# Block inversions in two groups of tiles, block moves by DMA, biases folded into weights, first tile of the last part by pairs

## The reference

```python
qkv = x @ gates_w + gates_b
q, k, v = jnp.split(qkv, 3, axis=-1)
lr = x @ lr_w + lr_b
k = k / jnp.linalg.norm(k, axis=-1, keepdims=True)
K = jnp.tril(jnp.einsum('ntc,nsc->nts', k, k), k=-1)
u = jax.scipy.linalg.solve_triangular(K + jnp.eye(T), v, lower=True)
score = jnp.einsum('nsk,ntk->nst', q, k)
y = jnp.einsum('nst,ntv->nsv', score, lr * u)
x = x + (y @ out_w + out_b)
x = x + relu(layernorm(x, mn_g, mn_b) @ w1 + b1) @ w2 + b2
```

## Time and profile before

| | us |
|---|---|
| median of 3 runs | 243.82 (243.53 to 244.35) |
| the profiled execution | 244.24 |
| its span in the profile | 242.4 |
| PE busy | 192.9 (80%) |
| DVE busy | 151.5 (62%) |
| ACT busy | 120.2 (50%) |
| POOL busy | 89.6 (37%) |

### The profile page before, as it was taken

How to read it: one execution, slowest core, us unless ns; L and a number is a source line. 1 busy time by engine, 2 the same in 40 slices (tenths; PEclk the granted TensorE clock), 3 DMA queues, 4 the chain that set the end, 5 groups by cost and what they waited for, 6 DMA issues and landing times.

```text
span 242.4 us, 4068 instructions
## 1 busy us (share of the span) xinstructions
PE 192.9 (80%) x1328; PEld 138.1 (57%) x1328; DVE 151.5 (62%) x626; ACT 120.2 (50%) x316; POOL 89.6 (37%) x146
## 2 busy tenths in 40 slices
PE   0499899560028799999997647999999999999981
PEld 0287777420027799889886326666565566556530
DVE  2647642899982354455540444597977869787875
ACT  2468686859412344455445145527364555545130
POOL 2538888200058815555300752201433414021120
PEclk9999999975555599999999958999999999999997
DMA  5940000000000000000000000000101001010111
GB/s 137 292 104 0 3 3 0 3 0 1 0 0 0 3 0 3 3 0 5 1 3 0 0 3 0 0 0 0 47 0 43 18 28 45 1 43 0 46 43 43
DMA packets 12133, 5.58 MB, mean 23 GB/s; under 512 B 1736, under 2 KB 12112, under 8 KB 12112
## 3 DMA queue, kind: packets, MB, share of 16 engines
q1 hardware_dynamic: 11536, 5.25, 7.8%
q10 hardware_dynamic: 576, 0.07, 0.2%
HBM read 3.22 MB, written 2.10 MB: 22 GB/s over the span
## 4 chain that ended last, share of the span: by engine, by line
PE 63%; DVE 16%; ACT 2%; issue 1%; POOL 0%; DVEq 0%
PE ps L1031 21%; PE ps L827 7%; PE ps L822 4%; DVE xi L613 4%; DVE prod L606 4%; PE ps L943 4%; PE ps L947 3%; PE ps L1008 3%; PE ps L937 3%; PE ps L951 3%; PE ps L1023 3%; PE ps L923 2%; PE ps L931 2%; DVE v_all L756 2%; PE ps L898 2%
## 5 line engine op out<-in xcount | busy, mean ns | idle before, releaser
L1031 PE MATMUL ps<-ewC,v_all 128*128 128x512 f32 x128 | 60.3, 595 | 0.8 <-DVE v_all L756 0.7
L756 DVE COPY_PREDICATED v_all<-mask,ps 128x256 f32<-128x256 int32 x112 | 48.8, 436 | 19.0 <-ACT v_all L500 11.9
L1031 PEld LDWEIGHTS ps<-ewC,v_all 128*128 128x128 f32 x128 | 22.1, 191 | 19.2 <-issue 16.5
L314 POOL TENSOR_TENSOR x_all<-x_all,v_all 128x512 f32<-128x512 f32 x7 | 8.9, 1271 | 58.1 <-ACT v_all L506 58.1
L272 POOL COPY tt_all<-dT_all 32x128 f32<-32x128 f32 x30 | 11.8, 392 | 26.7 <-DVE dT_all L618 24.9
L898 PE MATMUL ps<-tt_all,gg_all 32*32 32x32 f32 x128 | 5.2, 205 | 17.5 <-POOL tt_all L272 17.5
L306 POOL TENSOR_TENSOR h_all<-h_all,cb 128x512 f32<-128x512 f32 x8 | 10.1, 1267 | 17.4 <-DVE cb L685 17.4
L226 POOL TENSOR_SCALAR xh<-x_all,mv,rr 128x128 f32<-128x128 f32 x16 | 12.5, 793 | 9.6 <-DVE rr L557 9.1
L479 ACT ACTIVATE k_all<-h_all,nb,rr 128x128 f32<-128x128 f32 x32 | 13.7, 483 | 2.8 <-DVE nb L710 2.8
L898 PEld LDWEIGHTS ps<-tt_all,gg_all 32*32 32x32 f32 x128 | 4.3, 117 | 18.9 <-issue 18.3
L565 DVE TENSOR_TENSOR v_all<-ps,bv 128x512 f32<-128x512 f32 x8 | 5.5, 692 | 15.1 <-PE ps L844 15.1
(11 more groups left out here) (134 smaller groups left out, 453.4 us busy)
## 6 DMA issues: line engine op xcount, KB each, us to landing
x_all<-in_L_attn_x_dram SPq DMA_DIRECT2D x8, 256.0 KB, 4.5
out_dram<-x_all SPq DMA_DIRECT2D x7, 256.0 KB, 2.3
ew<-in_L_ffn_expert_w_dram SPq DMA_DIRECT2D x1, 512.0 KB
out_dram<-x_all SPq DMA_DIRECT2D x2, 128.0 KB, 1.8
wk<-in_L_attn_gates_w_dram ACTq DMA_DIRECT2D x1, 64.0 KB, 4.0
wvl<-in_L_attn_gates_w_dram SPq DMA_DIRECT2D x1, 64.0 KB, 3.8
bv<-in_L_attn_gates_b_dram SPq DMA_DIRECT2D x1, 64.0 KB, 3.4
b2s<-in_L_attn_b_dram SPq DMA_DIRECT2D x1, 64.0 KB, 4.1
```

The source lines that it names most:

```text
L756: nc.vector.copy_predicated(sel[t % 2][:, n], mask[t % 2][:, n, E - 1 - e].unsqueeze(2).broadcast_to([P, 2, F]), ps[:, b:b + 2, (e % EH) * ...
L1031: last = nc.tensor.matmul(ps[:, 4 + 2 * half + n, :], x1T[t % 2][:, 2 * pair + n], ewC[:, EH * half:EH * half + EH, :].rearrange("p e f -> ...
```

## The change

- Front: the values leave it. ACT takes one sequence of each normalised tile, POOL one and DVE two, into `h_all` (no double buffer). dn_g is multiplied into the weights (`gall`), dn_b and the biases become two small products added to the weights (`folded`) or a bias column of the keys (`kb`); the constant 1 is added to `xnT` so that the value bias comes out of the product itself. The first tile of x comes by two transfers.
- The diagonal blocks are moved by 28 transfers of SP from `gg_all` to `gd`, of tile 3 by four copies of ACT. POOL's `blocks`, `tt_` and `da_` are gone.
- The inversion runs in two groups, tiles 0 to 3 and 4 to 7. A group has 64 blocks, and each lies on two partitions, one for the even and one for the odd columns of its inverse, so a step is on (31-j) x (j//2+1) elements. The first group starts after tile 3; DVE's list has the second group's steps interleaved with the recurrence's first tiles.
- `v_` of all tiles, the preparation of the expert weights (`prep(0)` to `prep(3)`) and the joins of tiles 0 and 1 run on PE and ACT while DVE inverts; the first tile's right sides and all of these evictions are ACT's. `prep(4)` and `prep(5)` (the two centred expert products) stand in the fold.
- h is computed during the recurrence (ACT two sequences of a tile, POOL two), no longer during the inversion.
- Last learning-rate products straight from PSUM, two by ACT and two by DVE; the fold and the first tile of the last part by pairs of sequences (LOW, HIGH); the q bias through the weights, out_b as a product of one row; `cb` and `hcb_` are gone.

```diff
--- before.py
+++ after.py
...
-    def blocks(t):
...
-        for b in range(NB):
...
-            nc.gpsimd.tensor_copy(gd_all[r, :, t * NS:t * NS + NS].rearrange("p c n -> p n c"),
-                                  gg_all[r, t, :, Q * b:Q * b + Q]).then_inc(gd_done, 1)
...
-    def hcb_(t):
-        nc.gpsimd.tensor_tensor(h_all[:, t], h_all[:, t], cb[:], ALU.add).then_inc(hcb_ready, 1)
...
+    sp.dma_start(x_all[:, 0, 0:2], x_v[:, 0, 0:2]).then_inc(x_loaded[0], 16)
...
+    for t in range(T):
+        if t == TG - 1:
+            continue
+        sp.wait_ge(g_ready, t + 1)
+        for b in range(NB):
+            r = slice(Q * b, Q * b + Q)
+            sp.dma_start(gd[t // TG][r, t % TG * NS:t % TG * NS + NS, :],
+                         gg_all[r, t, :, Q * b:Q * b + Q]).then_inc(gd_sent[t // TG], 16)
...
+    pool.wait_ge(d_done, NG)
...
+    for t in range(T):
+        for n in LOW:
+            last = nc.gpsimd.tensor_scalar(h_all[:, t, n], x_all[:, t, n], mv[:, 0, t, n, 0:1], rr[:, t, 0, n:n + 1],
+                                           ALU.subtract, ALU.mult)
+        last.then_inc(h_pool, 1)
+        pool.wait_ge(h_pool, t + 1)
+        pool.wait_ge(h_act, t + 1)
+        nc.gpsimd.tensor_tensor(x_all[:, t], x_all[:, t], b2s[:, :].unsqueeze(1).broadcast_to([P, NS, C]),
+                                ALU.add).then_inc(xb2_ready, 1)
...
+    act.dma_start(x_all[:, 0, 2:4], x_v[:, 0, 2:4]).then_inc(x_half, 16)
...
-        nc.scalar.activation(rows(xnT_all[:, t]), ps[:, 0, :], ACT.Identity, bias=dnb, scale=dng).then_inc(xnT_ready, 1)
+        nc.scalar.activation(rows(xnT_all[:, t]), ps[:, 0, :], ACT.Identity, bias=onec[:, 0:1]).then_inc(xnT_ready, 1)
...
+        if t == TG - 1:
+            for b in range(NB):
+                r = slice(Q * b, Q * b + Q)
+                last = nc.scalar.copy(gd[0][r, t * NS:t * NS + NS, :], tiles(2 + t % 2)[r, :, Q * b:Q * b + Q])
+            last.then_inc(gd_act, 1)
...
+    nc.scalar.mul(gall[:, C:2 * C], wall[:, C:2 * C], dng).then_inc(scaled_k, 1)
...
+            nc.scalar.mul(bmean[:], dnb.broadcast_to([P, P]), 1.0 / C)
+            nc.scalar.mul(gall[:, 0:C], wall[:, 0:C], dng)
+            nc.scalar.mul(gall[:, 2 * C:3 * C + 1], wall[:, 2 * C:3 * C + 1], dng).then_inc(scaled_w, 1)
...
+    def diagonals(g):
+        act.wait_ge(dT_done, g + 1)
+        for b in (0, 2):
+            r = slice(Q * b, Q * b + Q)
+            nc.scalar.copy(by_block(tt_all, g, r, b), dT_all[g][r])
+        r = slice(0, Q)
+        nc.scalar.copy(by_block(da_all, g, r, 0), plain(g)[r]).then_inc(tt_act, 1)
...
+    for n in LOW:
+        act.wait_ge(w_mm, t * NS + n + 1)
+        nc.scalar.mul(ww[t % 2][:, n, C:2 * C], ps[:, n, C:2 * C], v_all[:, t, n, C:VW]).then_inc(lrw_ready, 1)
...
-    m, w = Q - 1 - j, j + 1
+    m, w = Q - 1 - j, j // 2 + 1
...
+        nc.vector.transpose(lt[:].rearrange("p c r -> p (c r)"),
+                            gd[g][:, :, :].rearrange("p t c -> p c t").unsqueeze(2).broadcast_to([P, Q, 2, GN])
+                            ).then_inc(lt_done, 1)
...
+    def place(g):
...
+        nc.vector.transpose(d_all[g][:].rearrange("p k l -> p (k l)"),
+                            xi[g][:].rearrange("p r k -> p k r")).then_inc(d_done, 1)
+        dve.wait_ge(d_done, g + 1)
+        nc.vector.transpose(dT_all[g][:].rearrange("p t r -> p (t r)"), plain(g)).then_inc(dT_done, 1)
...
+        nc.vector.tensor_copy(by_block(da_all, g, slice(Q, 2 * Q), 1), plain(g)[Q:2 * Q])
+        for b in (1, 3):
+            r = slice(Q * b, Q * b + Q)
+            last = nc.vector.tensor_copy(by_block(tt_all, g, r, b), dT_all[g][r])
+        last.then_inc(tt_dve, 1)
...
+    prepare(0)
+    eliminate(0, 0, Q - 1)
+    place(0)
+    prepare(1)
+    eliminate(1, 0, CUTS[0])
+    for n in range(NS):
+        s_(0, n)
...
+    for n in HIGH:
+        dve.wait_ge(w_mm, t * NS + n + 1)
+        nc.vector.tensor_scalar(ww[t % 2][:, n, C:2 * C], ps[:, n, C:2 * C], v_all[:, t, n, C:VW], None,
+                                ALU.mult).then_inc(lrw_last, 1)
...
+    def folded(dst, of, ready):
+        nc.tensor.matmul(dst, cent[:], gall[:, of], start=True, stop=False)
+        nc.tensor.matmul(dst, bmean[:], wall[:, of], start=False, stop=False)
+        nc.tensor.matmul(dst, oner[:], ball[:, of], start=False, stop=True).then_inc(ready, 1)
...
-    pe.wait_ge(mT_ready, 1)
...
-    nc.tensor.matmul(ps[:, 6, :], bqB[:], rows(mw[:, :, :]), start=True, stop=True).then_inc(cb_mm, 1)
-    nc.tensor.matmul(ps[:, 7, :], wqT[:], rows(mw[:, :, :]), start=True, stop=True).then_inc(gn_mm, 1)
+    for bank, of in ((7, LOW), (3, HIGH)):
+        nc.tensor.matmul(rows(tiles(bank)[:, span(of)]), oner[:], bor[:, :].unsqueeze(1).broadcast_to([1, 2, C]),
+                         start=True, stop=False)
+    for pair, of in enumerate((LOW, HIGH)):
+        pe.wait_ge(mT_ready, pair + 1)
+        four(5 + pair, lambda n: mT[:, n], lambda n: wo[:], mw_mm, of)
+    for pair, (bank, of) in enumerate(((7, LOW), (3, HIGH))):
+        pe.wait_ge(mw_ready[pair], 1)
+        nc.tensor.matmul(rows(tiles(bank)[:, span(of)]), wqT[:], rows(mw[:, span(of)]), start=False,
+                         stop=True).then_inc(gn_mm, 1)
...
```

1082 lines of the change are left out of this document (601 added, 481 removed).

## The result

The changed kernel takes **236.35 us** (median of four executions: 236.16, 236.18, 236.52 and 242.22) against 244.08 for the kernel before. The ratio is 0.969, 95% interval 0.966 to 0.972: 3.1% faster. The forecast was 224.9, with a range of 219.4 to 232.0: the direction is right, the size is not. The profiled execution has a span of 234.4, so 10.9 us are to be found against the 223.5 of the sum.

A forecast was written before the change was run, and what follows sets the result against it. GpSimd was taken to bound the front, VectorE the inversion, TensorE the recurrence and experts, dependent steps the fold. Span 242.4 - 14.5 (to w(3)) - 4.4 (fold) = 223.5; + 1.84 - 0.42 gave 224.9 us, range 219.4 to 232.0.

The forecast's parts named there:

- w(0) starts near 62.6: First tile's w products, after the joins of tiles 0 and 1: start at 62.6, its state reaching VectorE at 65.4.
- The cover: Joins and values hidden under VectorE's inversion steps: 0.6 us of slack; as a rival, 1 to 4 us late, chance 0.08.
- The clock rival: TensorE gaps from 50 to 86 keep the clock low until tile 3: 8 us more, 233; chance 0.09.
- Its second half, low through tile 7: Half clock holding through tile 7 of the recurrence as well: 19 us more, 252; chance 0.04.
- To tile 3: From the second placing's end to w(3): 5.6 us with handovers, w(3) at 85.9 instead of 100.43.
- The lt transposes: Start of each inversion group: transpose, reciprocal, scaling and one small instruction, 3.2 us for the first group, 3.3 the second.
- The placing: VectorE's transposes and three 32x512 copies after each group's inversion steps: 4.3 us, bounds 3.4 to 6.5.
- GpSimd's hold: GpSimd normalising h beside VectorE's second placing: 0.6 us added; rival 2 to 4 us more over some 23 us, chance 0.14.
- Periods of tiles 4 to 7: Recurrence tiles 4 to 7 keep TensorE's list of products, 6.68 us each, so w(7) starts at 112.6.
- Fold and first tile: From w(7) to the second expert group: 23.9 us against 28.28 by working in pairs, 4.4 gained.
- The front: Work up to the fourth tile: loop of 3.45 us per tile, first inversion starting at 27.1.
- The line for the steps: Inversion step cost: 0.28 us plus 4.7 ns per element of width, at least 0.46; 15.7 for 31 steps.

The follow-up runs named there:

- fill_first_gap: Changed kernel plus 14 filler products of 128x128 on TensorE between the third preparation and ya(0); 233.6 to 236.0 us, ratio 0.958.
- values_ahead: Changed kernel with value tiles 4 and 5 moved ahead of ya(0), 6 and 7 one step earlier; 233.4, 233.9, 234.3 us, ratio 0.952.
- in_order: values_ahead, tile3_by_scalare, blocks_in_a_row together, value tile 5's eviction behind the first yT copies, GpSimd copying the first diagonal block; 227.1 to 228.6 us, ratio 0.935.
- fill_second_gap: Changed kernel plus 8 filler products of 128x128 on TensorE in za(3), ahead of its wait for VectorE's yT copy; 231.6 to 233.2 us, ratio 0.949.
- tile3_by_scalare: Changed kernel with ScalarE, not VectorE, taking the yT copy and negated block of the third tile's join; 231.1 to 233.3 us, ratio 0.947.
- turns_alone: Changed kernel plus five more stream transposes on VectorE after the first placing, only to read their durations; 242.5 us.
- fold_order: Changed kernel with prep(5) moved behind tile 0's first transposes and tile 0's second-half expert products ahead of tile 1's hidden product; 235.5 and 235.6 us, ratio 0.959.
- in_order_filled: in_order plus 6 filler products of 128x128 on TensorE ahead of y64(3); 229.0 to 231.3 us, ratio 0.944.
- both_fillings_tile3: in_order_filled with values where the changed kernel has them and 10 filler products in the first gap instead; 228.3 to 230.2 us, ratio 0.941.
- before_filled: Kernel before the change plus 66 products of 128x128 on TensorE in the inversion, ahead of ya(0); 243.4 to 243.8 us, ratio 0.992.
- fill_joins_denser: Changed kernel with both gaps filled plus 23 filler products between the steps of the joins of tiles 0 and 1; 230.1 to 232.7 us, ratio 0.949.
- blocks_in_a_row: Changed kernel with GpSimd copying the inverted third diagonal block so za reads its weights unstrided; 235.0, 236.6, 236.7 us, ratio 0.964.
- after: The changed kernel as profiled, nothing further altered; 236.35 us median, span of the profiled execution 234.4.

## Why the prediction missed

*The step that failed* is "w(0) starts near 62.6". From ya(0) at 51 it counted 8 us of ScalarE's work and "some 3.5 of waits between the engines", 11.6 in all, and let TensorE's own work cost nothing beside them. Measured, ya(0) came at 51.9 and w(0) 16.0 later. ScalarE's work was right (7.4); its waits were 8.6 instead of 3.5. TensorE was the full engine, busy 15.86 of the 15.99 at a granted clock of 0.53, with 2.09 instead of 1.06 for three of the four value groups among the joins and 1.66 for the first. The earlier trace rows had the same joins at 0.50 for all 11.59 us, without the value groups; the forecast kept that for a rival of 0.09. fill_first_gap shows that the clock falls in these joins also when the gap ahead of them is filled. The right reading of the earlier trace rows was: where these joins run, the clock is low, and the change puts four wide groups between them.

*The cover* was called 0.6 thick and priced at "each us more on ScalarE". It was late by TensorE, not by ScalarE's work: 3.1 of idle VectorE, and 1.1 more, mostly in state copies and right sides that waited for half-clocked products. values_ahead brings the wait to 0.5 with the clock still at half, by taking wide products out of the stretch, and in_order closes it. How much of the 3.1 would go at full clock with the list as it is no run shows by itself.

*The clock rival* gave 233 with its 8 us up to tile 3. Measured: 3.1 + 1.1 here, if all of it is put down to the clock, 1.5 between the placing and w(3), 1.9 in tile 3's period, 7.6 in sum. That the size agrees so well is in part luck. Its reason, gaps of TensorE from 50 to 86, holds for the wait of 2.3 in za(3) (fill_second_gap); from 51 to 81 TensorE had hardly a gap and was at half clock to 73 all the same. Place and size were right, the mechanism half, and its chance was too low. Its second half, low through tile 7, did not come: from 97 on the clock was 1.00.

*To tile 3.* The 5.6 from the placing to w(3) were measured as 7.4. The sum had the order right (VectorE's copy for za(3) behind the placing, TensorE's states of tile 2 behind that copy), but took it at full clock, though TensorE stands idle there for 2.3 us. fill_second_gap takes 1.5 of the 1.8 away; tile3_by_scalare shows that the order itself costs 2.4 more.

*Terms of the right mechanism and a wrong size.* The lt transposes: taken as 1.25 like the earlier trace rows, measured 1.94 twice, 1.4 too little (turns_alone: the strided read, whose 1.86 stood in the trace before). The placing: 4.3 forecast, 3.65 measured without GpSimd beside it. GpSimd's hold: 0.6 allowed, 1.05 measured, once and not over the 23 us that its rival feared. Periods of tiles 4 to 7: 6.68 forecast, 6.88 measured, 0.8 in four; "keep TensorE's list of products" overlooked that one of them reads its weights in stride. Fold and first tile: 4.4 forecast, 3.65 measured. The front: 27.1 against 27.78, where the forecast's own terms (23.5, 0.7, 1.0, 1.55) add up to 26.8. The line for the steps, 0.28 plus 4.7 ns per element, misses one of the two rows that it is drawn from (0.89 for a width of 130, where the row has 0.79) and gives some 16.6 for 31 steps; that the 15.7 beside it was met (15.64) is not that formula's merit.

*What was right.* 31 steps of the first group in 15.6, cheaper by their width; the 28 small transfers at no cost (1.8 us to landing, as taken from the earlier trace rows); the expert part within 0.3; the preparations ahead of the first transposes of the fold, which held them up by 1.2 (1.5 forecast; fold_order), though only 0.4 of it reached the hidden product.

VectorE's first transpose of the inversion and what it waited for, and the row of the transfers:

```profile
27.78 1.94 DVE L696 STREAM_TRANSPOSE lt<-gd 128x1024 f32<-128x1024 f32 x1 [0.96 <-ACT gd L363]
...
gd<-gg_all SPq DMA_DIRECT2D x28, 16.0 KB, 1.8
```

On the rule of the Trainium skill weighed there (DMA: Bandwidth & Descriptors, section Bandwidth): the figures that the rule stands under are of transfers from HBM, and small as these transfers within the SBUF are, they landed in time; the first lt transpose waited for ScalarE's last copy, not for them, so the rule cost nothing here.

*Sum of the 10.9:* front 0.7; transposes and placing together 0.6; idle VectorE and the slower copies behind it, up to the placing, 4.2; placing -0.2; to w(3) 1.8; tile 3's period by the clock 1.9; strided weights 0.8; fold 0.7; rest and rounding 0.4.

What stays open: why the clock falls in the joins at all with waits of 0.3, why it stays down there through 14 us of a full TensorE (fill_first_gap) and comes back in the products of tile 0; and why the same wait does not always bring a fall. Ahead of ya(4) TensorE waits 1.0 in the profiled executions of in_order_filled (230.4) and of both_fillings_tile3 (228.3), with the same lists there; in the first the clock was at 0.58 from 86 to 90, in the second at 1.00.

## What to carry over

When the trace before shows a stretch at half clock, take the half clock as that work's price until a row shows the same work at full clock, and price whatever is moved into it at that rate too. A wait placed behind a long instruction list on another engine (VectorE's placing here) costs its length and then the clock; ask for each wait on the path what is queued ahead of it. Move real work in the lists before adding filling: it gained as much at the first gap (233.4 to 234.3 against 233.6 to 236.0) and leaves nothing in the way, whereas filling ahead of y64(3) made in_order slower (227.1 to 228.6 became 229.0 to 231.3). And read an operand's stride before taking over a row's duration.

## What was not expected of the hardware

- The clock fell at 57 in fill_first_gap after 5 us in which TensorE was busy 4.47 and waited 0.3 at most at a time, and stayed down for 14 us of full occupation. 15 us of 128x128 products in a row kept it at 1.00 (before_filled), and with 23 such products among the joins two executions had a mean of 0.998 (fill_joins_denser).
- A stream transpose of 1024 elements takes 1.25 in a row and 1.92 at a stride of 32 elements; of 512 elements 0.71 and 1.09. Reading each element twice costs nothing more (turns_alone).
- Four 32x32 weights read at a stride cost TensorE 0.2 us per tile (6.88 against 6.67, blocks_in_a_row).
- VectorE's two 32x512 copies and GpSimd's two normalisations lengthen one another when they meet: VectorE's by 1.05 us and GpSimd's by 0.27 in after, only GpSimd's, by 0.73, in blocks_in_a_row.
